# Column strips for the side products and transposes of two fused recurrences

## What is computed

```python
# layer 0: a tanh recurrence over the 512 tokens
h = tanh(xp[t] + h @ Wh)                                # Wh 256 x 256
# layer 1: an LSTM over the 512 tokens
a = xW[t] + h @ Wh                                      # Wh 256 x 1024
c = sigmoid(a_f) * c + sigmoid(a_i) * tanh(a_g)
h = sigmoid(a_o) * tanh(c)
# layer 2: hyperbolic attention and feed-forward, modulated by ada = cond @ w_ada + b_ada
xm = expmap0(layer_norm(logmap0(x)) * (1 + sc_msa) + sh_msa)
q, k, v = (to_heads(expmap0(logmap0(xm) @ w + b)) for w, b in ((w_q, b_q), (w_k, b_k), (w_v, b_v)))
...                                                     # attention, output product, Mobius additions, feed-forward
# layer 3: two of four experts per sequence and a shared one
```

## Time and profile before

| | |
|---|---|
| Time, median of 3 executions | 2486.86 us (2485.87 to 2488.44) |
| The profiled execution | span 2483.3 us, 96145 instructions; its own total is not listed apart |
| TensorE: matmuls, weight loads | 2358.1 us (95%), 1570.9 us (63%) |
| VectorE, ScalarE, GpSimd | 1570.9 us (63%), 1350.9 us (54%), 569.8 us (23%) |
| Granted TensorE clock, mean | 0.991 |
| The 520 slots | from the start to about 1183 us |

### The profile page before, as it was taken

One profiled execution on the slowest core, in us unless ns is written; L12 is line 12 of the kernel. 1 busy time (PEld: TensorE's weight loads), 2 busy tenths in 40 slices (PEclk: granted clock), 3 DMA queues, 4 the chain that ended last, 5 costly groups with the idle time before them and its releaser, 6 DMA issues.

```text
span 2483.3 us, 96145 instructions
## 1 busy us (share of the span) xinstructions
PE 2358.1 (95%) x39648; PEld 1570.9 (63%) x39648; DVE 1570.9 (63%) x7207; ACT 1350.9 (54%) x4515; POOL 569.8 (23%) x1177
## 2 busy tenths in 40 slices
PE   8899999999999999999868999999999999999999
PEld 6677777777777777776333665646556465564666
DVE  5777777777777877777466546546465464655330
ACT  4555555555555555555748556565555665556432
POOL 0222222332223222232222203222031221212100
PEclk9999999999999999999979999999999999999999
DMA  4111111110000000000103002030020301102020
GB/s 114 33 36 42 32 40 42 32 30 25 30 27 29 27 27 30 26 23 15 65 0 115 1 14 110 0 124 1 33 92 1 124 1 52 72 1 98 1 81 9
DMA packets 51880, 102.74 MB, mean 41 GB/s; under 512 B 10468, under 2 KB 33380, under 8 KB 47348
## 3 DMA queue, kind: packets, MB, share of 16 engines
q1 hardware_dynamic: 48036, 94.06, 11.2%
q10 hardware_dynamic: 3408, 2.52, 0.3%
HBM read 75.53 MB, written 21.04 MB: 39 GB/s over the span
## 4 chain that ended last, share of the span: by engine, by line
PE 42%; DVE 4%; ACT 3%; issue 2%; POOL 1%; DVEq 0%; ACTq 0%
PE bank L1262 13%; PE bank L1276 12%; PE bank L1470 4%; PE bank L1478 4%; ACT pexp L2032 2%; PE bank L1383 2%; PE bank L1368 1%; PE bank L1435 1%; PE bank L1297 1%; POOL hs L2111 1%; PE bank L1353 1%; PE bank L1314 1%; DVE x L1595 0%; DVE x L1598 0%; DVE spl L1786 0%
## 5 line engine op out<-in xcount | busy, mean ns | idle before, releaser
L135 PE MATMUL psFI<-wh,Hs 128*8 128x128 f32 (+3 forms) x8192 | 324.8, 276 | 60.5 <-DVE Hs L250 47.1
L135 PE MATMUL psOR<-wh,RH 128*16 128x128 f32 (+3 forms) x8320 | 321.4, 272 | 2.5 <-ACT RH L338 2.1
L135 PEld LDWEIGHTS psFI<-wh,Hs 128*8 128x8 f32 (+3 forms) x8192 | 182.2, 99 | 178.9 <-DVE Hs L250 178.4
L2032 ACT ACTIVATE pexp<-bank 128x1024 f32<-128x1024 f32 x256 | 244.2, 1022 | 33.8 <-PE bank L1368 33.6
L338 ACT ACTIVATE RH<-RT 128x16 f32<-128x16 f32 x512 | 111.0, 217 | 261.3 <-DVE RT L254 261.3
L1262 PE MATMUL bank<-x3T,ew 128*128 128x512 f32 x512 | 239.2, 594 | 0.0
L329 ACT ACTIVATE sFI<-FIT 128x32 f32<-128x32 f32 x512 | 118.6, 232 | 200.3 <-DVE FIT L234 195.5
L234 DVE STREAM_TRANSPOSE FIT<-psFI 128x128 f32<-128x128 f32 x512 | 162.3, 317 | 101.0 <-PE psFI L135 98.5
L135 PEld LDWEIGHTS psOR<-wh,RH 128*16 128x16 f32 (+1 forms) x8320 | 205.6, 104 | 5.1 <-ACT RH L338 3.7
L135 PE MATMUL psG<-wh,Hs 128*8 128x64 f32 (+3 forms) x8192 | 208.3, 219 | 0.0
L1276 PE MATMUL bank<-ew,hidden 128*128 128x256 f32 x864 | 201.0, 379 | 0.0
(11 more groups left out here) (358 smaller groups left out, 4631.3 us busy)
## 6 DMA issues: line engine op xcount, KB each, us to landing
ew<-in_ew SPq DMA_DIRECT2D x32, 1024.0 KB, 9.6
qkv_scratch<-qkvr SPq DMA_DIRECT2D x31, 384.0 KB, 2.7
big<-qkv_scratch SPq DMA_DIRECT2D x7, 1536.0 KB, 7.6
XX<-in_xT SPq DMA_DIRECT2D x31, 256.0 KB, 2.7
x_scratch<-xr SPq DMA_DIRECT2D x32, 128.5 KB, 2.4
x<-x_scratch SPq DMA_DIRECT2D x8, 514.0 KB, 8.8
ada<-ada_scratch SPq DMA_DIRECT2D x8, 512.0 KB, 8.4
out_x<-x SPq DMA_DIRECT2D x7, 512.0 KB, 3.3
```

The lines of the kernel that those rows point to most:

```text
L135: last = pe.matmul(bank[32 * j:32 * j + width, :], state(k), weights[:, k, j, cols], start=False, stop=k == KC - 1, tile_position=(0, 32 * ...
L2032: up(act.activation(M.pexp[:, n % 2, 2 * pr:2 * pr + 2, :], M.PS[pr][:, :, :], ACT.Exp, scale=1.0 / math.sqrt(HD)), "exps")
```

## The change

A helper `strips` makes four matmuls with 32 of the 128 stationary columns each, placed on the four column strips of the array and writing the four quarters of the PSUM partitions. The transposes of x2 and of zr and the products with wqkv go through it. The transposes thereby become ordinary matmuls with the identity as the moving operand. Order, waits and signals stay, and the last strip raises the semaphore. Behind the loop (`last_rows_back`, `last_normed`, `last_products`) nothing changes.

```diff
--- before.py
+++ after.py
@@ -727,6 +727,12 @@
 
 
     def tensor_engine(self, pe, x2, x2_made):
+        def strips(out, stationary, moving, start, stop):
+            for j in range(4):
+                at = slice(32 * j, 32 * j + 32)
+                last = pe.matmul(out(at), stationary[:, at], moving, start=start, stop=stop, tile_position=(0, 32 * j), skip_group_check=True)
+            return last
+
         def slot(i):
             if i in (10, 11):
                 k = i - 10
@@ -758,7 +764,7 @@
                         if c >= 2:
                             pe.wait_ge(*self.at("zT_out", c - 2))
                     columns = self.psA[:, 0:D].rearrange("p (j k u) -> p j k u", k=KC, u=32)[:, :, o, :]
-                    last = pe.transpose(columns, x2(c)[:, o, :], self.W.I[:, :])
+                    last = strips(lambda j: columns[j], x2(c)[:, o, :], self.W.I[:, :], True, True)
                     if o == 1:
                         self.raise_(last, "xT")
                 if o in (18, 19):
@@ -766,7 +772,7 @@
                     if k == 0:
                         pe.wait_ge(*self.at("z", c))
                         pe.wait_ge(*self.at("xT_out", c + 1))
-                    last = pe.transpose(self.psA[:, k * P:(k + 1) * P], self.z[:, k * P:(k + 1) * P], self.W.I[:, :])
+                    last = strips(lambda j: self.psA[j, k * P:(k + 1) * P], self.z[:, k * P:(k + 1) * P], self.W.I[:, :], True, True)
                     if k == 1:
                         self.raise_(last, "zT")
                 if 20 <= o < 32:
@@ -779,8 +785,8 @@
                             pe.wait_ge(self.wqkv_in, 16 * 9)
                         if c or n:
                             pe.wait_ge(*(self.at("qkv_out", c, n) if n else self.at("qkv_out", c - 1)))
-                    last = pe.matmul(self.psB[:, half * P:(half + 1) * P], self.zT[:, k, :], self.wqkv[:, k, n * D + half * P:n * D + (half + 1) * P],
-                                     start=k == 0, stop=k == KC - 1, skip_group_check=True)
+                    last = strips(lambda j: self.psB[j, half * P:(half + 1) * P], self.zT[:, k, :], self.wqkv[:, k, n * D + half * P:n * D + (half + 1) * P],
+                                  k == 0, k == KC - 1)
                     if half and k:
                         self.raise_(last, "qkv")
         return slot
```

## The result

The changed kernel takes 2492.3 us (median of 15 runs, 2489.5 to 2495.1) against 2487.2 us for the kernel before, run beside it on the same chip (15 runs, 2485.9 to 2488.9). The ratio is 1.0019, 95% interval 1.0011 to 1.0027: slower by 5.1 us. Measured again beside other kernels it was 1.0026 (1.0015 to 1.0037). So the change costs about 0.2%, just where the prediction had set the border of "no change", and on the slow side of it.

The account below looks back on a forecast made before the run. The prediction took the recurrences to be bound by a 2.28 us loop in which TensorE waits for VectorE's Hs. The 130 us freed on TensorE lay outside it, so 2483.3 + 0 profiled, median 2486.9 unchanged; range 2482 to 2492.

Parts of the forecast that it names:

- no change: Whole kernel: time stays at 2487 us, within 5 us; 88%, made of the forecast's 80% and 8% for a remaining gap.
- the slow rival: TensorE's instruction queue: late instructions stall the loop, 24 x 0.57 = 13.7 us, deciding from 9 stalls (5 us); 7%.
- "issue" on L135: TensorE's waits in the recurrences: if its loads at L135 waited for instructions, the forecast would be wrong.
- the case that the steps stand: Recurrences: if steps keep their length but the time moves, the cause lies in the second half; check its clock first.
- What sets the pace: Recurrences: a loop through TensorE, VectorE and ScalarE, 2.28 us a step; TensorE waits for Hs in all 495 steps.
- The rival in which TensorE sets the pace: Recurrences: the freed 130 us are gained in full, 2357 us; 5% together with a smaller case of 5 to 10 us.
- The price of the strips: Products and transposes in the recurrences: four strips take 0.22 us, saving 0.31 us per product and 0.15 us per transpose.
- The bound of 1.3 us: Products in the recurrences: upper limit if four strips don't overlap, costing 0.6 us per step, about 2700 us; 1%.
- The gap of 0.20 us: Ahead of full-array loads at L782: idle for "issue" 344 times, 70.4 us, taken as the drain on changing tiling mode.
- the rival in which it stays there: Ahead of the first strip: the gap has another cause and remains, still inside the unused time, 2487 us; 8%.
- Nobody else waits for the moved ends: End of the slot: ScalarE's copies and VectorE's scaling come after TensorE has gone on, so earlier ends gain nothing.
- I cost them at nothing: the cover is the unused 0.5 us per step: TensorE's instruction queue: 6028 added records, some 24 packets, cost 0 us because idle time each step covers them.

Follow-up runs that it names:

- e3_records: The kernel before with three small fp32 matmuls into spare columns of psB ahead of each of the 360 full-array products, 4320 records more: 2489.7 against 2486.4 us.

## Why the prediction was right in its range, and where it failed

The time fell on the upper edge of the range: 2492.3 us by the measured median, 0.3 above it, and 2491.6 by the measured ratio on the 2486.9 us that the prediction started from. It is slower where no change was the likeliest, and the change of 0.19% stands at the border of the case with 88%. The likeliest number, 2487, was 5 us low. That the time still fell at the edge of the range is owed to the slow rival, up to whose deciding point the range was drawn, and not to the sum, which came to 0. Of the signs that the prediction named, the one against it came true ("issue" on L135), and the place that it named for the case that the steps stand, the second half, was the wrong one: the median step is 2.27 us before and after, and a few long ones among them make the 4.8 us.

- *What sets the pace*: right. 2.25 to 2.28 us a step before and after, and the run without the products' time is no faster. The rival in which TensorE sets the pace is refuted.
- *The price of the strips*: right. Forecast 0.66 us from OR block to inputs' block, measured 0.65; forecast a wait for Hs of about 300 us, measured 304.2. The bound of 1.3 us was not needed.
- *The gap of 0.20 us*: gone in front of the strips, so the rival in which it stays there falls. In e3_records the full-array load comes 0.58 us after the OR block's first matmul, about as before, with small strips in between; that fits a load that has to wait for the block ahead of it to run out, and nothing tested it further.
- *Nobody else waits for the moved ends*: right as far as the traces show.
- *"I cost them at nothing: the cover is the unused 0.5 us per step"*: this is the step that failed. The count was right (24 packets forecast, 23 measured). The cover was not. What is unused lies behind the inputs' block, and TensorE stands there at a wait for Hs, so it cannot run ahead into the next step's FI, G and OR blocks. When a packet is late within one of these three, 96 of the 144 records of a changed step, the loop is late by up to as much, however long TensorE idled before. The timeline at 411.36 us shows the delay; that TensorE cannot run ahead is how I read it. The unused time covers only a packet that is late in the product or in the inputs' block, and of that no more than its own length: in front of the strips one wait of 1.52 us ended at 536.71 us, and the next gates' load began at 537.13 without waiting for Hs, which had been written from 536.21 to 536.38.
- *The rival of late instructions*: its place and mechanism were right; 7% was too little for it. Its price was not: it put a stall at 0.57 us and asked for 9; measured are 13 and 21 on L135, of 0.41 and 0.30 us each on average, some of them in the inputs' block, where the unused time takes them up. I took the absence of such waits in the kernel before as evidence against. It was evidence for one rate of records only, with 4.37 us between packets. How near that was to what the queue can bring was not asked. The other argument against it, DMA engines that are busy a tenth of the time, doesn't rule it out: of the 14 edges with a wait in the changed kernel, five had no data packet on the DMA engines since the edge before.

## What to carry to other kernels

An edit that trades TensorE's time for more instructions is free only if both can be spared. Before it is made, take the distance between packets of the instruction queue over the stretch and see whether any block on the critical chain already waits for "issue"; where such waits stand, or the blocks' edges come nearly as close as in the runs here that lost time (4.3 us and less apart in the median, where the kernel before had 4.4), fewer and wider matmuls are worth more than shorter ones. And a slack that ends in a wait on a semaphore doesn't protect what is queued behind that wait.

## What the runs showed of the hardware that was not expected

- TensorE's late instructions come at one place modulo 256 records, all 166 of those counted above. The time lost grows far faster than the records: +6028 cost 5 to 6 us, +10348 cost 43 us, and the packets then started every 3.91 us.
- TensorE's instructions came one packet ahead and no more: in all twelve profiles there is one packet for each edge, none starts more than 0.6 us before the edge ahead, and no edge is passed sooner than 2.15 us after its packet's start.
- How much of the lateness the data transfers make is open; no run moved or removed them. One wait was traced to a stretch of 3.8 us with data on 57.7% of the DMA engines and no packet of instructions. Over the whole trace of the changed kernel they are not needed for a wait, but go with the long ones: of its 14 waits five have no data packet between the edge and the one before, the longest of them 0.48 us, and in front of the three of 0.9 us and more data held 22 to 51% of the DMA engines.
- Four loads of the kernel without the products' time waited for "issue" with no record added. Whether a faster TensorE alone brings this on was not settled.
